# A two-layer graph network on one core: final states loaded during the drain, and relation rows from one fp32 product

## The reference, cut to what matters

```python
feat = (h @ W).reshape(N, 2, 64)                       # layer 0, once
e = leaky_relu(el[src] + er[dst], 0.2)
alpha = softmax of e over the edges of each dst
x = x + layernorm(segment_sum(feat[src] * alpha, dst) + bias) * gamma + beta
agg = entity = relu(layernorm(x))                      # layer 1
for _ in range(3):
    h, t, rel = agg[head], agg[tail], edge_emb[edge_type]      # 64 relations
    att = sum((h @ q_w) * tanh(rel * t @ k_w))
    w = softmax of att over the edges of each head
    agg = segment_sum(w * rel * t, head) / max(count, 1)
    agg = agg / max(norm(agg), 1e-12)
    out = out + agg + entity
return x + out
```

## Time and profile before

| what | us |
|---|---|
| median of 3 runs (lowest to highest) | 9809.54 (9796.19 to 9809.73) |
| the profiled execution | 9807.02 |
| its span | 9805.2 |
| busy PE, DVE, ACT, POOL in the span | 8923.7, 7921.7, 7321.4, 6810.7 |

### The profile page before, as it was taken

How to read it: one execution, slowest core, us unless ns; L and a number is a source line. 1 busy time by engine, 2 the same in 40 slices (tenths; PEclk the granted TensorE clock), 3 DMA queues, 4 the chain that set the end, 5 groups by cost and what they waited for, 6 DMA issues and landing times.

```text
span 9805.2 us, 277571 instructions
## 1 busy us (share of the span) xinstructions
PE 8923.7 (91%) x65693; PEld 7235.6 (74%) x65693; DVE 7921.7 (81%) x33650; ACT 7321.4 (75%) x23591; POOL 6810.7 (69%) x7059
## 2 busy tenths in 40 slices
PE   7996777777776999999997999999997999999997
PEld 6985666666664777777775777777775777777775
DVE  7898999999997777777775777777775777777775
ACT  2204999999996777777775777777775777777775
POOL 1336777777775777777775777777775777777775
PEclk9998999999997999999998999999998999999998
DMA  2003444444444555555556555555556555555556
GB/s 49 5 12 82 108 109 109 109 109 109 109 109 115 159 159 159 159 159 158 159 159 133 158 160 160 157 159 159 159 159 140 159 159 159 159 159 159 159 159 122
DMA packets 1133743, 1308.57 MB, mean 133 GB/s; under 512 B 452629, under 2 KB 847723, under 8 KB 1133325
## 3 DMA queue, kind: packets, MB, share of 16 engines
q1 hardware_dynamic: 899446, 841.26, 28.0%
q0 software_dynamic: 229008, 460.45, 21.1%
q10 hardware_dynamic: 5126, 4.76, 0.2%
HBM read 1041.61 MB, written 260.45 MB: 133 GB/s over the span
## 4 chain that ended last, share of the span: by engine, by line
PE 63%; DMA 10%; DVE 9%; issue 8%; POOL 7%; ACT 3%; SPq 1%; DVEq 0%; POOLq 0%; ACTq 0%
PE bank L737 52%; DMA agg<-agg_d,arena 6%; POOL agg L705 6%; PE bank L897 5%; PE bank L882 5%; PE bank L850 2%; DMA agg<-feat_d,arena 2%; DVE agg L1545 2%; DVE agg L1555 2%; ACT arena L1011 2%; DVE arena L1535 1%; POOL wide L718 1%; DMA arena<-type_d 1%; DVE arena L1513 1%; DVE arena L1504 0%
## 5 line engine op out<-in xcount | busy, mean ns | idle before, releaser
L705 POOL DMA_INDIRECT agg<-agg_d,arena x5124 | 4852.1, 947 | 1731.1 <-issue 1432.1
L1655 DVE TENSOR_TENSOR arena<-agg,bank 128x256 f32<-128x256 f32 x2562 | 1080.2, 422 | 1451.1 <-PE bank L737 1064.4
L705 POOL DMA_INDIRECT agg<-feat_d,arena x1708 | 1618.3, 947 | 529.4 <-issue 421.4
L737 PE MATMUL bank<-arena 128*128 128x129 f32 x10248 | 1825.6, 300 | 32.6 <-ACT arena L1090 30.5
L737 PE MATMUL bank<-tmp,wide 128*128 128x256 f32 x5124 | 1540.1, 383 | 10.1 <-DMA wide<-left_d 10.1
L737 PE MATMUL bank<-tmp,kw_s 128*128 128x256 f32 x5124 | 1532.9, 381 | 0.0
L737 PEld LDWEIGHTS bank<-arena 128*128 128x128 f32 x10248 | 1338.5, 190 | 211.3 <-issue 43.3
L1086 ACT ACTIVATE arena<-arena 128x1 f32<-128x1 f32 x2562 | 754.6, 295 | 931.7 <-DVE arena L1519 890.6
L1081 ACT ACTIVATE arena<-agg,arena 128x256 f32<-128x256 f32 x2562 | 1337.9, 522 | 57.8 <-DVE arena L1648 52.2
L1094 ACT ACTIVATE tmp<-bank 128x256 f32<-128x256 f32 x2562 | 982.1, 383 | 427.6 <-PE bank L737 372.6
L1648 DVE CUSTOM_DVE_ANT_0 agg<-bank,arena 128x256 f32<-128x256 f32 x2562 | 1228.6, 480 | 19.6 <-issue 8.0
(11 more groups left out here) (242 smaller groups left out, 17251.0 us busy)
## 6 DMA issues: line engine op xcount, KB each, us to landing
state_d<-arena SPq DMA_DIRECT2D x488, 455.0 KB, 2.7
arena<-key_d SPq DMA_DIRECT2D x489, 448.0 KB
arena<-type_d SPq DMA_DIRECT2D x367, 448.0 KB
wide<-left_d SPq DMA_DIRECT2D x2562, 64.0 KB
agg<-agg_d,arena POOLq DMA_INDIRECT x5124
agg<-feat_d,arena POOLq DMA_INDIRECT x1708
arena<-er_d SPq DMA_DIRECT2D x854, 1.0 KB
arena<-peers SPq DMA_DIRECT2D x489, 7.0 KB
```

What stands on the lines that cost most here:

```text
L705: nc.gpsimd.indirect_dma_start(out=rows_r[:, k % R, c, 0:width], out_offset=None, in_=table, in_offset=bass.IndirectOffsetOnAxis(ap=peer_r ...
L737: return nc.tensor.matmul(out, lhsT, rhs, start=start, stop=stop)
L1655: V.tensor_tensor(val_r[:, j % R, :, 0:F], rows_r[:, j % R, :, 0:F], bank[0][:, 0:G].rearrange("p (c f) -> p c f", c=2), ALU.mult).then_in ...
```

## The change

1. **States in four parts, during the drain.** `PARTS` become 18, 17, 7 and 7 blocks. Groups are in the order of blocks and each block has at least one, so the last group of block b lies at least 48 - b groups ahead of the end: blocks 0 to 17 are stored two bodies before the end, 18 to 34 one body, 35 to 41 half a body. SP loads its share (10, 9, 3 and 3 blocks) at fixed steps of the drain body, each behind a wait on the stores it needs. POOL (8, 8, 4 and 2) does so behind its last gather. ACT keeps 2 blocks of the last part.
2. **Room for it.** `left_r` moves in `wide` behind the first 35 states (`EARLY`), so parts 0 and 1 have a free place; parts 2 and 3 wait until the last scores have read `left_r`. `PART_WORDS` grows to 18 blocks.
3. **Order at the border.** SP stores the four parts of `agg` first, then the left rows in four pieces. DVE makes all four `directions` before any `add_hop`. ACT does both large squares first, loads the root's table ahead by an activation on `root_junk`, and takes the later roots between left tiles. POOL's next loop waits for 4 turned tiles and one `add_hop` in place of 6 and 2.
4. **Relation rows.** One fp32 product per half with the 64 rows of `emb_s`; `hot_r` is fp32 with a ring of 2, types are loaded to 64 partitions, and the nine operations of `pack(14)` and one load go.
5. **A fill.** Ahead of the first loop SP writes numbers into the last 14 groups of `state_d` (three DMAs from `giota`, 932 KB) and waits for them.

The diff, cut to its core:

```diff
-PARTS = ((0, 12), (12, 24), (24, 36), (36, NB))
-ACT_LOADS = (range(0, 4), range(12, 16), range(0), range(0))
-POOL_LOADS = (range(4, 8), range(16, 20), range(24, 30), range(36, 42))
-SP_LOADS = (range(8, 12), range(20, 24), range(30, 36), range(42, NB))
-TILES_OF = (range(0, 3), range(3, 6), range(6, 9), range(9, LB))
-PART_WORDS = 13 * F
+EARLY = 35
+PARTS = ((0, 18), (18, EARLY), (EARLY, 42), (42, NB))
+POOL_LOADS = (range(0, 8), range(18, 26), range(35, 39), range(42, 44))
+SP_LOADS = (range(8, 18), range(26, 35), range(39, 42), range(44, 47))
+SP_FIRST = 2
+ACT_LOADS = range(47, NB)
+TILES_OF = (range(0, 4), range(4, 8), range(8, 10), range(10, LB))
+LEFTS = ((0, 16), (16, 32), (32, 40), (40, NB))
 HALVES = ((0, 24), (24, NB))
 HALF_AT, ROOT_AT = (0, 8), (0, 3)
 BATCH = 3 * F
 BATCHES = 13
 SIGNS_AT, TOTALS_AT = 12, 68
 TABLES_AT = (84, 88, 92, 96)
+PART_WORDS = 18 * F
...
-        spaces = {"arena": [arena[:], 0, ARENA], "agg": [agg_flat, 0, NB * F], "tmp": [tmp_flat, 1024, NB * F], "wide": [wide[:], 0, NB * TW]}
+        spaces = {"arena": [arena[:], 0, ARENA], "agg": [agg_flat, 0, NB * F], "tmp": [tmp_flat, 1024, NB * F], "wide": [wide[:], EARLY * SW, NB * TW]}
...
-        hot_r = ring((R, G), BF16)
+        hot_r = ring((2, G))
...
-                            sp.dma_start(flat(type_r), row(type_d).partition_broadcast(P)).then_inc(d, 16)
+                            sp.dma_start(flat(type_r)[0:RELS], row(type_d).partition_broadcast(RELS)).then_inc(d, 16)
...
+                    if b.last and k == 0:
+                        for i in range(2):
+                            sp.wait_ge(q["stored"][i], b.landed("stored", i * R - 3 * U))
+                        load_states(layer, 0, SP_LOADS[0])
+                        for i in range(2):
+                            sp.wait_ge(q["stored"][i], b.landed("stored", i * R - 2 * U))
+                        load_states(layer, 1, SP_LOADS[1][0:SP_FIRST])
+                    if b.last and k == STORE[layer] - R:
+                        load_states(layer, 1, SP_LOADS[1][SP_FIRST:])
+                        sp.wait_ge(q["stored"][0], b.landed("stored", -U))
+                        apart(sp)
+                        if layer == 1:
+                            sp.wait_ge(q["scores_ready"], b.count(-1))
+                        load_states(layer, 2, SP_LOADS[2])
...
+            sp.wait_ge(rowid_made, 1)
+            for at in range(0, U * SW, NG):
+                n = min(NG, U * SW - at)
+                sp.dma_start(state_d[:, (NG - U) * SW + at:(NG - U) * SW + at + n], giota[:, 0:n]).then_inc(tail_finite, 16)
+            sp.wait_ge(tail_finite, 3 * 16)
...
-                store_agg(0)
-                store_agg(1)
-                store_left(0)
-                store_agg(2)
-                store_left(1)
-                store_agg(3)
-                store_left(2)
-                store_left(3)
+                for part in range(4):
+                    store_agg(part)
+                for part in range(4):
+                    store_left(part)
...
+                def stored(bodies):
+                    for i in range(2):
+                        pool.wait_ge(pipes[layer]["stored"][i], 16 * bodies[i] if h is None else pool.snap(h * (16 * BODIES) + 16 * bodies[i]))
+                    apart(pool)
+
                 for part in range(4):
+                    stored(((BODIES - 2, BODIES - 2), (BODIES - 1, BODIES - 1), (BODIES, BODIES - 1), (BODIES, BODIES))[part])
+                    if part == 2 and layer == 1:
+                        pool.wait_ge(pipes[1]["scores_ready"], pool.snap(h * NG + NG))
+                        apart(pool)
...
-                pool.wait_ge(aggT_ready, pool.snap(hop * LB + 6))
-                pool.wait_ge(xs_done, pool.snap(hop * 4 + 2))
+                pool.wait_ge(aggT_ready, pool.snap(hop * LB + 4))
+                pool.wait_ge(xs_done, pool.snap(hop * 4 + 1))
...
-                        mm(bank[0][:, c * P:(c + 1) * P], hot_r[:, j % R, c * P:(c + 1) * P], emb_pair[:], True, False)
-                        last = mm(bank[0][:, c * P:(c + 1) * P], hot_r[0:RELS, j % R, c * P:(c + 1) * P], emb_low[:], False, True)
+                        last = mm(bank[0][:, c * P:(c + 1) * P], hot_r[0:RELS, j % 2, c * P:(c + 1) * P], emb_s[:])
...
+                for b in ACT_LOADS:
+                    g = act.value_load(lastg[layer][0:1, b:b + 1], min_val=0, max_val=NG - 1)
+                    act.dma_start(wide[:, b * SW:(b + 1) * SW], state_d[:, bass.ds(g * SW, SW)]).then_inc(state_in[3], 16)
...
+                nc.scalar.activation(root_junk[:], rowid[:, 0:1], ACT.Sqrt)
+                square_of(1)
+                load_states(1, hop)
                 length_of(0)
-                square_of(1)
+                length_of(1)
+                square_of(2)
+                square_of(3)
                 for part in range(4):
                     for t in TILES_OF[part]:
+                        if t == 2:
+                            length_of(2)
+                        if t == 5:
+                            length_of(3)
...
-                elif n == 14:
-                    do(V.tensor_copy(emb_high[:], emb_s[:]))
-                    do(V.tensor_tensor(emb_rest[:], emb_s[:], emb_high[:], ALU.subtract))
-                    do(V.tensor_copy(emb_pair[0:RELS], emb_high[0:RELS]))
-                    do(V.tensor_copy(emb_pair[RELS:2 * RELS], emb_rest[RELS:2 * RELS]))
-                    do(V.tensor_copy(emb_high[0:RELS], emb_rest[0:RELS]))
-                    do(V.tensor_tensor(emb_s[0:RELS], emb_rest[0:RELS], emb_high[0:RELS], ALU.subtract))
-                    do(V.tensor_copy(emb_low[:], emb_s[0:RELS]))
-                    do(V.tensor_scalar(rel_row[:], rowid[:, 0:1], RELS - 0.5, -float(RELS), ALU.is_ge, ALU.mult))
-                    do(V.tensor_tensor(rel_row[:], rel_row[:], rowid[:, 0:1], ALU.add))
...
-                    V.tensor_scalar(hot_r[:, j % R, :], type_r[:, j % U, :], rel_row[:, 0:1], None, ALU.is_equal)
+                    V.tensor_scalar(hot_r[0:RELS, j % 2, :], type_r[0:RELS, j % U, :], rowid[0:RELS, 0:1], None, ALU.is_equal)
...
                 lengths(0)
+                lengths(1)
                 directions(0)
-                for part in range(1, 4):
-                    lengths(part)
-                    add_hop(part - 1)
-                    directions(part)
-                add_hop(3)
+                lengths(2)
+                directions(1)
+                lengths(3)
+                directions(2)
+                directions(3)
+                for part in range(4):
+                    add_hop(part)
```

50 lines of the change are left out of this document (18 added, 32 removed).

## The result

| what | us |
|---|---|
| changed kernel, median of 4 runs | 9940.3 (9927.1 to 9943.6) |
| kernel before, median of 4 runs | 9804.8 (9796.2 to 9809.7) |
| ratio, 95% interval | 1.014 (1.0128 to 1.0153) |
| span of the profiled execution, before and after | 9805.2 and 9941.8 |

A forecast was written before the change was run, and what follows sets the result against it. POOL's gathers, 2.50 us a group, bound the loops just above PE's 2.48; DMA jam and borders add waits. From 9809.5, -52 - 13.5 - 4 - 2 - 7.5 = -79 gave 9730 us; range 9703 to 9768, own range 9705 to 9752.

The forecast's parts named there:

- the part on the loops: Hop loops: fp32 pair at 0.54 us, PE's step 2.39 us under POOL's 2.50; -2 us, and -7.5 us from halved types.
- Rival 3: Hop loops: PE becomes the bound and slower once the fp32 pair costs more than 0.65 us; chance 0.04.
- Its own case of 0.75 us: Hop loops: fp32 pair at 0.75 us makes the step 2.60; 2562 groups add 256 us, giving 9986.
- The rule of four passes: PE's fp32 products make four array passes each; at bf16 price the pair takes 1.26 us, lengthening the kernel by 1560 us.
- The borders between hops: Two borders between hops: early loads fit, directions end T + 23.8, POOL starts T + 29; 26 us each, -52 us.
- Rival 1: Borders behind hops: early loads jam the drain, the stores come late, 8 us at each of three, 9754; chance 0.12.
- the sign that the forecast gave for it: Borders: a store of states late by more than 2 us behind DVE's last sum.
- The last border: From the last hop's drain to the span's end: T + 42 in place of T + 55.7, -13.5 us (-8 to -18).
- Behind layer 0: Border behind layer 0: DVE's 6.9 us wait for states goes, smaller last store; -4 us, bounds +3 and -9.
- The start: Ahead of the first gathers: nine DVE operations less give -2 us, the fill costs +2 (0 to 6); together 0.
- The jam: End of hop loops: DMA engines 99.5% taken, read without proof as padding groups all fetching one row slowly.
- Rivals 2 and 4: Hops: late left rows make POOL wait, 9754, chance 0.08; borders did not wait for the loads, 9780, chance 0.04.

The follow-up runs named there:

- the kernel of 3: The whole change, its fp32 relation product contracting over 128 rows (rows 64 to 127 zeros), against the kernel before: ratio 0.9971.
- 8: Borders, bf16 rows, spread padding: 9679.0 us, ratio 0.9871 to the kernel before; from this base, without early loads in the hops 9723.4 us, with alternating stores ratio 0.9885.
- 2: The fp32 relation pair alone, put into the kernel before: ratio 1.0196, +190 us.
- 7: Padding gathers rows 0 to 127: change with 128-row fp32 product 0.9907, borders with bf16 rows 0.9877, kernel before alone 9715.6 us (0.9908), all against the kernel before.
- 5: The change's borders with bf16 relation rows, `emb_low` padded with zeros so all four products have 128 rows, against the kernel before: ratio 0.9956.

## Why the prediction was wrong

**The step that failed** is in the part on the loops: "The new pair has the shape of the first, so PE's step falls to 2.39 us." It holds two mistakes. The shapes differ in the one thing that decides, 64 rows against 128. And the row taken as the price, 0.54 us, was not clean: that pair stands behind `emb_low` with its 64 bf16 rows and carried some 0.10 us for its neighbours, about half of it for the change of rows. Behind fp32 products of 128 rows it is 0.45. The measured sum is 2.20 us for a step with fp32 pairs over 128 rows, plus 0.38 for two changes: 2.58, in place of 2.39. With it falls the step behind it, that PE stays under POOL's 2.50 us and its time is worth nothing. That decided 204 us, because the margin to POOL was 0.02 us a step. The forecast had that margin in its first part, and gave the case in which it is passed a chance of 0.04. Why a change of rows costs PE time is not shown; that it does, and how much, is.

**Rival 3 was the right one**, with its threshold: from 0.65 us on, PE is the bound. Counted as it counts, 2.58 - (2.48 - 0.63), the pair costs 0.73 us, and 0.08 us over 2.50 in 2562 groups on top of 9730 is 9935; 9940 came. Its own case of 0.75 us gave 9986. What spoke for it was named (only 64 rows, which no fp32 row shows). What spoke against it was misread: `emb_low` takes 0.16 us "like `emb_pair`" because both pay for a change, not because rows are free. Two equal durations in an alternating pair show nothing of either.

**The rule of four passes** (the Trainium skill, FP8 and Floating Point Precision, TensorE Precision Notes) was weighed with the price of 0.157 us and set aside, since the pair then came to 1.26 us. At the clean price of 0.055 us eight passes are 0.44 us, and the pair with 128 rows takes 0.45. The rule agrees with the trace; the price was wrong.

**The borders between hops** were right: -49.9 us for -52. Step by step: directions ended at T + 24.4 (forecast T + 23.8), the next gather started at T + 30.6 (T + 29). The gather came 6.2 us behind the last directions, where 5.2 were counted for the store. Rival 1 was right in its mechanism and cost next to nothing here: SP's 12 early loads took 18.57 us, 1.55 each for the 1.06 assumed, and the last store of states came at T + 2.1 in place of T + 0.3, which just meets the sign that the forecast gave for it. (Ten loads stand between the two stores, not the seven of its text.) In the kernel of 3 the same mechanism costs 3 to 7 us a border. The reason given for the gain, loads that no longer stand behind T, is what 8 shows: 14 to 15 us a border. But 8 has spread padding, where all of the new border is worth 17 us behind T; here it is 24.6 (55.2 - 30.6), with a drain that the stall makes longer, as the forecast's 26 us had it. How much of the 24.6 us the early loads bring was not measured.

**The last border**: -15.0 for -13.5. **Behind layer 0**: -5.4 for -4. Both inside their bounds. **The start** cost 6.3 us where +2 - 2 = 0 was taken. The nine operations less save about 0.5 us (831.3 us ahead of the first gather in 2, against 831.8), not 2. The fill was put at +2 with 6 as its bound; the other kernels that have it start 2.6 to 5.5 us later than the kernel before, so part of the 6.3 is scatter.

**The jam**: "My reading, which no row proves, is that the padding groups all fetch one row, and slowly" was right, as 7 shows. That halved types would give 2.5 us a hop of it was too much: loops with types for 64 partitions (3) and for 128 (5) differ by 5 us in all three hops together, and the product differs too.

**Rivals 2 and 4** fall: POOL waited for no indices early in a loop, and the borders between hops shrank by 28 and 22 us. The forecast's own range of 9705 to 9752 is not half of its bounds, which gives about 9716 to 9749; with 9940 measured this decides nothing.

## What to carry to other kernels

Before a duration from one place is used for an instruction in another, look at its neighbours on the engine: on this one, products over 64 rows between products over 128 cost 0.10 to 0.19 us at each change, and filling the operand up with rows of zeros, or putting like beside like, made them cheaper. Where two engines are within 1% of each other, a simplification on the faster one needs a measured price, and the loss multiplies by the number of steps, while a border is gained once.

Padding should not gather one address: spread over 128 rows, it took 87 us off the kernel before, and 67 off the one with the new borders, since the two gains overlap. The version that beats both kernels has the borders of the change, the bf16 rows of the kernel before and spread padding: 9679 us, ratio 0.9871 (0.9855 to 0.9888).

## What the runs showed of the hardware that was not expected

- A change between products over 64 and over 128 rows costs 0.10 to 0.12 us beside bf16 products (PE's steps of 2.48, 2.27 and 2.03 us with 4, 2 and 0 changes) and 0.19 us beside fp32 ones (2.58 and 2.20 us with 2 and 0). 256-column products ahead hide none of it: their pair takes 0.52 us in place of 0.43.
- A bf16 product of 128 columns with fresh weights takes 0.055 us of PE between its like, an fp32 one 0.22 to 0.23.
- Gathers of one row over and over cost 0.77 us a packet on the mean of the loop's last 60 us, gathers of spread rows 0.13 us.
- A gather of POOL takes 0.952 us on the mean in loops in which PE is idle for part of each step, and 0.947 us where PE's step is 2.48; the cause is open.
- In the hop loops of kernels in which PE is idle for part of each step, the granted clock fell to half for some 20 short stretches a hop (0.98 on the mean of a loop with a step of 2.20 us); with PE's step at 2.48 us it stayed at 1.00.
